# A gather kernel for a recommendation model: one field of five tiles fetched row by row from SyncE's queue, and layers and last steps in another order

## The reference

```python
sp_emb = emb_tables[fidx, sp_input]                      # 2048 x 26 x 32
lin_vals = lin_tables[fidx, sp_input, 0]
lin_output = ds_input @ lin_w.T + lin_b + jnp.sum(lin_vals, axis=1, keepdims=True)
s = jnp.sum(sp_emb, axis=1)
bi_pooled = 0.5 * (s * s - jnp.sum(sp_emb * sp_emb, axis=1))
x = jnp.concatenate([bi_pooled, ds_input], axis=1)       # 2048 x 45
h = jax.nn.relu(x @ w1.T + b1)                           # 256
h = jax.nn.relu(h @ w2.T + b2)                           # 128
out = jax.nn.sigmoid(h @ fw.T + fb + lin_output)
```

## Time and profile before

| | |
|---|---|
| median of 3 runs | 400.91 us (400.11 to 402.16) |
| the profiled execution, own time | 398.72 us |
| its span, first to last instruction | 396.9 us |
| mean granted TensorE clock | 0.993 |
| busy share: TensorE products, VectorE, GpSimd, ScalarE | 95%, 83%, 73%, 61% |
| gathers from GpSimd | 300, mean 956 ns |
| matching products | 1624 |

### The profile page before, as it was taken

One profiled execution on the slowest core, in us unless ns is written; L12 is line 12 of the kernel. 1 busy time (PEld: TensorE's weight loads), 2 busy tenths in 40 slices (PEclk: granted clock), 3 DMA queues, 4 the chain that ended last, 5 costly groups with the idle time before them and its releaser, 6 DMA issues.

```text
span 396.9 us, 5382 instructions
## 1 busy us (share of the span) xinstructions
PE 378.9 (95%) x1766; PEld 324.6 (82%) x1766; DVE 329.0 (83%) x336; ACT 240.3 (61%) x406; POOL 287.8 (73%) x310
## 2 busy tenths in 40 slices
PE   3999999999999999999999999999999988999884
PEld 2888888888888888888888888888888875767542
DVE  6799999979789796997979799697978995485952
ACT  5996865876376673875639756477665465322222
POOL 5777777777777777777777777777777777777740
PEclk9999999999999999999999999999999998999998
DMA  7733236332543327333273223633254222222210
GB/s 226 191 80 29 27 33 184 34 26 14 139 85 27 28 15 194 28 28 29 14 195 27 27 29 43 178 30 26 15 140 69 14 14 14 14 15 14 14 12 0
DMA packets 16900, 23.01 MB, mean 58 GB/s; under 512 B 6084, under 2 KB 15958, under 8 KB 15961
## 3 DMA queue, kind: packets, MB, share of 16 engines
q0 software_dynamic: 9600, 5.09, 22.9%
q1 hardware_dynamic: 7272, 17.58, 13.9%
HBM read 22.60 MB, written 0.04 MB: 57 GB/s over the span
## 4 chain that ended last, share of the span: by engine, by line
PE 92%; DVE 4%; ACT 2%; issue 1%; DMA 1%; ACTq 0%
PE cand L704 42%; PE cand L707 42%; PE bank_b L743 1%; PE bank_b L736 1%; PE bank_b L725 1%; PE bank_b L749 1%; PE bank_b L718 1%; PE bank_b L756 1%; DMA idx_raw<-sparse 1%; DVE sums L420 1%; PE cand L743 1%; PE cand L736 1%; ACT gates L562 1%; DVE last_picks L384 0%; DVE pick_sums L407 0%
## 5 line engine op out<-in xcount | busy, mean ns | idle before, releaser
L301 POOL DMA_INDIRECT rows<-table,row_idx x300 | 286.7, 956 | 94.1 <-issue 70.7
L704 PE MATMUL cand<-high,gates 128*128 128x462 f32 x812 | 308.3, 380 | 0.4 <-DVE gates L352 0.4
L707 PE MATMUL cand<-low,gates 128*128 128x462 f32 x812 | 304.2, 375 | 0.0
L704 PEld LDWEIGHTS cand<-high,gates 128*128 128x128 f32 x812 | 154.4, 190 | 23.2 <-issue 5.0
L707 PEld LDWEIGHTS cand<-low,gates 128*128 128x128 f32 x812 | 154.0, 190 | 20.4 <-issue 2.4
L384 DVE TENSOR_REDUCE picks<-masked 128x66 f32<-128x924 f32 x56 | 107.4, 1917 | 1.9
L378 DVE TENSOR_TENSOR masked<-cand,mask 128x924 f32<-128x924 f32 x57 | 63.7, 1118 | 42.3 <-PE cand L707 42.0
L562 ACT ACTIVATE gates<-distance,one 128x512 fp32r<-128x512 bf16 x116 | 76.9, 710 | 0.0
L554 ACT ACTIVATE distance<-codes,minus_key 128x512 bf16<-128x512 f16 x112 | 74.4, 712 | 0.0
L352 DVE TENSOR_SCALAR gates<-bank_a,key_of 128x512 fp32r<-128x512 f32 x87 | 59.9, 743 | 0.5 <-ACT bank_a L548 0.5
L529 ACT CAST high<-stage 128x462 fp32r<-128x462 f32 (+2 forms) x52 | 31.0, 596 | 33.4 <-DMA stage<-tabs 33.3
(11 more groups left out here) (91 smaller groups left out, 99.1 us busy)
## 6 DMA issues: line engine op xcount, KB each, us to landing
stage<-tabs SPq DMA_DIRECT2D x7, 1617.0 KB
rows<-table,row_idx POOLq DMA_INDIRECT x300, 3.2
codes<-codes_dram SPq DMA_DIRECT2D x28, 128.0 KB, 3.1
stage<-tabs SPq DMA_DIRECT2D x7, 231.0 KB, 4.2
idx_raw<-sparse SPq DMA_DIRECT2D x1, 208.0 KB, 2.5
w_sb<-w2t SPq DMA_DIRECT2D x1, 128.0 KB
xT<-dense_rows SPq DMA_DIRECT2D x1, 120.0 KB
w_sb<-w1x SPq DMA_DIRECT2D x1, 80.0 KB
```

The costliest lines, as they stand in the source:

```text
L301: pool.indirect_dma_start(out=rows[t % RING][:, g * W:(g + 1) * W], out_offset=None, in_=table[:, :], in_offset=bass.IndirectOffsetOnAxis( ...
L704: first = nc.tensor.matmul(to, gate, high[f % 2][:, k, :], start=(k == 0), stop=False)
L707: last = nc.tensor.matmul(to, gate, low[f % 2][:, k, :], start=False, stop=(k == CHUNKS - 1))
```

## The change

One field of tiles 3, 6, 8, 11 and 13 (the last one, field 25) is no longer gathered from GpSimd, so 295 gathers are left (`PF` counts them for each tile). SyncE fetches it instead, one sample's row at a time: 128 direct DMAs of 33 floats for a tile, with the row's number read into a register. They stand in pieces of 26 behind the loads of codes of jobs 5 to 28, and two more pieces behind the last load: 25 pieces, 640 DMAs. VectorE works out the row numbers in three small instructions at the start, from a sixth small input of 5 x 128 numbers. ScalarE and VectorE wait for a second semaphore at each tile. Apart from that, ScalarE's order in jobs 26 to 28 and the order of the last steps on ScalarE, VectorE and TensorE are other ones, and the last tile's rows are cut after 13 of 18 fields and no longer after 15. The rule that holds gathers back keeps its numbers.

```diff
+    BY_ROW = [3, 6, 8, 11, 13]
+    PF = [GF[t] - (t in BY_ROW) for t in range(TILES)]
+    ROWS_AT = [5, 11, 16, 21, 26]
+    TURN_ROWS = 26
...
-    SPLIT = GF[LAST] - 3
+    SPLIT = GF[LAST] - 5
...
+            sp.dma_start(one_raw[:, :], singles).then_inc(one_in, 16)
             sp.wait_ge(codes_out, 16)
...
+            def load_rows(n, p0):
+                t = BY_ROW[n]
+                if p0 == 0:
+                    sp.wait_ge(one_step, 3)
+                    if t >= RING:
+                        sp.wait_ge(reduced, 2 * (t - RING + 1))
+                p1 = min(p0 + TURN_ROWS, P)
+                _, at = nc.values_load_multi_w_load_instructions(
+                    one_idx[n:n + 1, p0:p1], engines=[mybir.EngineType.SP], min_val=0, max_val=F * CATS - 1,
+                    skip_runtime_bounds_check_because="one_idx is clamped")
+                for p in range(p0, p1):
+                    sp.dma_start(rows[t % RING][p:p + 1, PF[t] * W:GF[t] * W], table[bass.DynSlice(at[p - p0], 1), :]
+                                 ).then_inc(one_by_one[t % RING], 16)
+            turns = {ROWS_AT[n] + p0 // TURN_ROWS: (n, p0) for n in range(len(BY_ROW)) for p0 in range(0, P, TURN_ROWS)}
...
                     load_codes(j)
+                    if j in turns:
+                        load_rows(*turns[j])
+            for j in range(NJ, max(turns) + 1):
+                load_rows(*turns[j])
...
-                for g in range(GF[t]):
-                    n = sum(GF[:t]) + g
+                for g in range(PF[t]):
+                    n = sum(PF[:t]) + g
...
+            dve.wait_ge(one_in, 16)
+            nc.vector.tensor_scalar(one_wrap[:, :], one_raw[:, :], 0, CATS, ALU.is_lt, ALU.mult).then_inc(one_step, 1)
...
                     dve.wait_ge(gathered[t % RING], gathered_until(t))
+                    dve.wait_ge(one_by_one[t % RING], rows_until(t))
...
                 act.wait_ge(gathered[t % RING], gathered_until(t))
+                act.wait_ge(one_by_one[t % RING], rows_until(t))
```

More of the change, by code:

```diff
@@ L5, with build_deep_fm @@
 from contextlib import ExitStack
-def build_deep_fm(nc, dense_rows, sparse, cols, table, tabs, w1x, w2t, b2c, fwc, wlx, out):
+def build_deep_fm(nc, dense_rows, sparse, cols, singles, table, tabs, w1x, w2t, b2c, fwc, wlx, out):
     fp32 = mybir.dt.float32
@@ L84, in build_deep_fm, with rows_until @@
     LAST = TILES - 1
-    SPLIT = GF[LAST] - 3
+    SPLIT = GF[LAST] - 5
     def gathered_until(t):
-        return 16 * sum(GF[u] for u in range(t % RING, t + 1, RING))
+        return 16 * sum(PF[u] for u in range(t % RING, t + 1, RING))
+    def rows_until(t):
+        return 16 * P * sum(u in BY_ROW for u in range(t % RING, t + 1, RING))
     def codes_until(j):
@@ L104, in build_deep_fm @@
     LET = [0] + list(itertools.accumulate(19 if j in HIDDEN else 12 for j in range(NJ) for _ in range(TB * len(HALVES))))
-    assert 10 * AHEAD + LET[-1] > 10 * sum(GF)
+    assert 10 * AHEAD + LET[-1] > 10 * sum(PF)
     def begun_until(n):
@@ L137, in build_deep_fm @@
         col_code = sb("col_code", [R, P], fp16)
+        one_raw = sb("one_raw", [len(BY_ROW), P], i32)
+        one_wrap = sb("one_wrap", [len(BY_ROW), P], i32)
+        one_idx = sb("one_idx", [len(BY_ROW), P], i32)
         codes = [sb(f"codes{k}", [P, N], fp16) for k in range(3)]
@@ L220, in build_deep_fm @@
         gathered_end = sem("gathered_end")
+        one_in = sem("one_in")
+        one_step = sem("one_step")
+        one_by_one = [sem(f"one_by_one{k}") for k in range(RING)]
         squared = sem("squared")
@@ L479, in _ @@
             make_mask(0, 1)
+            dve.wait_ge(one_in, 16)
+            nc.vector.tensor_scalar(one_wrap[:, :], one_raw[:, :], 0, CATS, ALU.is_lt, ALU.mult).then_inc(one_step, 1)
+            dve.wait_ge(one_step, 1)
+            nc.vector.scalar_tensor_tensor(one_wrap[:, :], one_raw[:, :], CATS - 1, one_wrap[:, :], ALU.min,
+                                           ALU.add).then_inc(one_step, 1)
+            dve.wait_ge(one_step, 2)
+            nc.vector.tensor_scalar(one_idx[:, :], one_wrap[:, :], 0, (F - 1) * CATS, ALU.max,
+                                    ALU.add).then_inc(one_step, 1)
             for j in range(NJ - 1):
@@ L513, in _ @@
             pick_last(2)
+            dve.wait_ge(gathered[LAST % RING], gathered_until(LAST) - 16 * (GF[LAST] - SPLIT))
+            sum_rows(LAST, LAST, 0, SPLIT)
             pick_last(3)
@@ L517, in _ @@
             relu1(BLOCKS - 1, 1)
-            dve.wait_ge(gathered[LAST % RING], gathered_until(LAST) - 16 * (GF[LAST] - SPLIT))
-            sum_rows(LAST, LAST, 0, SPLIT)
             dve.wait_ge(gathered_end, 16 * (GF[LAST] - SPLIT))
@@ L642, in _ @@
                     high_chunk(*CHUNK_AT[j, 0])
+                if j in HIDDEN:
+                    relu1(HIDDEN[j], 0)
                 if j - 1 in SUMMED_OF:
                     square_picks(SUMMED_OF.index(j - 1))
-                if j + 2 < NJ:
+                if j in HIDDEN:
+                    relu1(HIDDEN[j], 1)
+                elif j + 2 < NJ:
                     make_gates(j + 2, FIRST_ACT, ACT_GATES)
-                if j in HIDDEN:
-                    relu1(HIDDEN[j], 0)
                 if j in CASTS:
@@ L656, in _ @@
                     high_piece(f, PIECE[g], PIECE[g + 1])
-                if j in HIDDEN:
-                    relu1(HIDDEN[j], 1)
                 if (j, 1) in CHUNK_AT:
@@ L663, in _ @@
                 if j in HIDDEN:
+                    if j + 2 < NJ:
+                        make_gates(j + 2, FIRST_ACT, ACT_GATES)
                     relu2(HIDDEN[j])
@@ L668, in _ @@
             relu1(BLOCKS - 2, 0)
-            square_last(0, 2)
             relu1(BLOCKS - 2, 1)
             square_tile(LAST - 1)
+            square_last(0, 2)
             relu2(BLOCKS - 2)
             square_last(2, 3)
+            act.wait_ge(gathered[LAST % RING], gathered_until(LAST) - 16 * (GF[LAST] - SPLIT))
+            square_rows(LAST, LAST, 0, SPLIT)
             sigmoid(BLOCKS - 2)
@@ L677, in _ @@
             relu1(BLOCKS - 1, 0)
[L678 to L681, removed]
             act.wait_ge(gathered_end, 16 * (GF[LAST] - SPLIT))
             square_rows(LAST, LAST + 1, SPLIT, GF[LAST])
+            relu2(BLOCKS - 1)
             square_sums(BLOCKS)
+            sigmoid(BLOCKS - 1)
             relu1(BLOCKS, 0)
@@ L715, in turn, with turn_picks @@
             def turn(m, t, parts):
+                turn_picks(m, t)
+                return turn_rows(m, t, parts, parts[-1])
+            def turn_picks(m, t):
                 c = slice(t % TB * P, (t % TB + 1) * P)
@@ L722, in turn, with turn_rows @@
                     nc.tensor.matmul(TOTAL[m][0:V, c], last_picks[:, i, :], ident[:, :], start=False, stop=False)
+            def turn_rows(m, t, parts, end_of):
+                c = slice(t % TB * P, (t % TB + 1) * P)
                 for at in parts:
@@ L725, in turn @@
                     last = nc.tensor.matmul(TOTAL[m][0:V, c], sums[:, at, :], ident[:, :], start=False,
-                                            stop=(at == parts[-1]))
+                                            stop=(at == end_of))
                 return last
@@ L806, in _ @@
             linear(3)
-            layer2(3)
-            layer3(3)
             pe.wait_ge(y_made, BLOCKS - 1)
             pe.wait_ge(picked, PAIRS + 1)
-            turn(4, LAST, [LAST, LAST + 1]).then_inc(folded, 1)
+            turn_picks(4, LAST)
+            turn_rows(4, LAST, [LAST], LAST + 1)
+            layer2(3)
+            turn_rows(4, LAST, [LAST + 1], LAST + 1).then_inc(folded, 1)
+            layer3(3)
             layer1(4, 0)
@@ L846 @@
         "cols": np.ascontiguousarray(sp[:, :M].T).reshape(M * (B // P), P),
+        "singles": np.ascontiguousarray(sp[:, F - 1].reshape(B // P, P)[[3, 6, 8, 11, 13]]),
         "table": both.reshape(F * C, E + 1),
```

## The result

| | before | the change |
|---|---|---|
| median of 6 runs | 400.83 us | 450.75 us |
| ratio, 95% interval | | 1.124 (1.121 to 1.127) |
| profiled execution, own time; span | 398.72; 396.9 us | 450.94; 448.8 us |
| first fold of block 0 to the last `sigmoid` | 75.8 us | 70.2 us |

The account below looks back on a forecast made before the run. It took TensorE, 95% busy, as the bound, with GpSimd's gathers a second chain as long. Terms of -4.9, -1.5 and -2.2 us made -8.6 us, from 400.91 to 392.3 us, range 389.5 to 404.

Parts of the forecast that it names:

- Terms 1 and 2: Jobs 26 and 28: `relu1` ahead of gates and of the squares of `last_picks` shortens TensorE's waits; -4.9 and -1.5 us.
- the end of the products: Job 28 on TensorE: the last matching product ends at 373.3 us instead of 379.7.
- Term 3: Gathers and last steps at the kernel's end: five gathers less and the new order save 2.2 us.
- The price on SyncE: SyncE's list: 26 rows at 0.37 us plus a 1.0 us load make a 10.6 us piece, which fits, costing nothing.
- rival A: SyncE becomes the bound and tables come late; the gain is eaten at 12.0 us a piece; slower, chance 0.21.
- its formula: Table lateness from field 3 to field 7 for pieces of T us: 17 T - 187; beyond 9 us TensorE pays.
- That small transfers cost nothing: 640 one-row DMAs beside GpSimd's gathers: transfers overlap, so they were costed at nothing.
- the limit for late tables: Tables for ScalarE: up to 9 us late is made up by idle time on ScalarE and VectorE, costing nothing.
- the point where SyncE stops fitting: SyncE's list of four jobs against 47.13 us between table loads: stops fitting at a piece of 11.3 us.

Follow-up runs that it names:

- fixed rows: The change with 640 one-row fetches of constant row numbers, no register loads or address steps (field 25's look-up left out): 390.00 us against 400.69 before.
- ScalarE's order alone: The kernel before with only ScalarE's order in jobs 26 to 28 changed, last steps as before, 300 gathers: 394.64 us against 400.58.
- layers and last steps: The kernel before with the change's whole order of layers and last steps, last tile cut after 13 fields, no row fetches: 398.82 us against 400.69.
- even pieces: The change with pieces of 28, 28, 24, 24 and 24 rows, so register loads begin at multiples of 16 bytes: 420.88 us, ratio 1.050 to before.
- the kernel with three tiles: The change with only tiles 3, 6 and 12 by row, in pieces of 24 or 20 rows, 297 gathers: 396.24 us against 400.69 before.
- the kernel with four tiles: The change with tiles 5, 8, 11 and 14 by row from job 10 on, pieces of 24 or 20, 296 gathers: 393.28 us against 400.58 before.

## Why the prediction was wrong

**Terms 1 and 2 and the end of the products** were right where the tables are in time. With fixed rows the folds of blocks 0 and 2 stand 38.2 us apart (318.79 to 356.95; 43.0 before), and the products end at 373.0, forecast 373.3. The last `sigmoid` came 9.3 us earlier than before, forecast 8.6. ScalarE's order alone brought 5.9 us.

**Term 3** came out in the rows of the kernel with fixed rows, where the last gather starts at 375.2; no run had 295 gathers with the old last steps, so what the new ones are worth there is not shown. What I had not seen is that it is a loss without them: from 394.6 (layers alone) to 398.8 us (layers and last steps) with 300 gathers. I wrote that less than term 3 would remain if only the products ended earlier; it was less than nothing for the new order of the last steps, some 2.7 us of it by the clock level.

**The price on SyncE is the step that failed**, by two terms of its sum. I took a row at 0.37 us: 0.228 and 0.04 came as taken, but the address step was 0.14 us in place of 0.10, for there are two instructions, the second of which I had not counted. That is 1.0 us a piece. And I took the load of registers at 1.0 us: it was 1.6 to 2.0 us where it starts at a multiple of 16 bytes and 5.5 where not, 3.3 in the mean, 2.3 us a piece more. The rest of the difference are rows at up to 0.43 us. The upper bound of 3.2 us for this load was wrong too, as 5.5 lies far above it. The bounds of a whole piece (7 and 24 us) held; the value between them, 10.6, was 14.3. The mechanism stood in rival A with its place (the tables), the point at which it decides (12.0 us a piece) and a chance of 0.21. With 14.3 its formula gives 56 us of lateness at field 7 and some 439 us; 66 us and 450.75 were measured. With the even pieces' 12.6 us it gives 27 us and 410.5 us; 37 us and 420.88 were measured. So it has the slope right (29 us for 1.7 us a piece, 29.9 measured) and is 10 us too low in both. Of the 10 us of lateness that it lacks in the change, 5 were there at field 3 already, as field 2's table was 11.3 us late and the formula begins with one wait at field 3; 3.1 more are a second wait, which it does not have, of the piece of tile 11 for VectorE to sum tile 7 (until 255.7). That the rows alone would have turned the sign is not shown: at 0.41 us with a load of 1.0 they make a piece of 11.7 us, below the formula's 12.0, but the formula is too low where it can be checked.

**That small transfers cost nothing** was right (fixed rows, 0.974), and so was the limit for late tables in its order of size: 8.4 us late cost 3.3 us, so that 9 us for nothing was too generous. In the change itself this limit decided little, since the tables were 11 to 66 us late.

The rule of the Trainium skill that I weighed ("DMA: Bandwidth & Descriptors", section "Why a DMA increments its semaphore by 16 and not by 1", 512 sequencer cycles for a DMA instruction on generations before the newest; with the 1.2 GHz of "Advanced Engine Details and Errata", "Clock Domains", an estimate of 0.43 us) reached the right sign for a reason that the trace does not bear out: the issue took 0.228 us. The Trainium skill's page "DMA: Bandwidth & Descriptors", section "Latency and other measured facts", gives about 600 ns as the floor of a tensor load. This case agrees that it is a floor: 1.38 us were the least for 20 registers, in the kernel with three tiles. I had left it out of the sum, where 0.6 in place of 1.0 would have made the piece shorter still.

The chance was the weaker choice. My value for a piece lay 0.7 us below the point where SyncE stops fitting and 1.4 below the one that decides the sign, and two of its three unknown terms were hardly bounded at all (0 to 0.3 us for the address step, 0.04 to 3.2 us for the load). That is nearer to an even chance than to 0.21.

## What to carry to other kernels

When work moves to an engine that "only issues DMAs", write that engine's list as a budget per period and count every instruction of it, register loads and address arithmetic too; one that fills 94% of the period on guessed prices, as here (44.2 of 47.13 us), can as well be the bottleneck. Measure the load of registers before its price goes into a sum, and let it start at multiples of 16 bytes. And an order of last steps is worth what the arrival times make it: the one that belongs to the 390.0 us with 295 gathers lost 4 us with 300, so such moves are to be tried apart.

## What the runs showed of the hardware

- A load of registers from SBUF on SyncE took 1.39 us for 20, 1.61 for 24 and 1.84 for 28, some 0.056 us a register. For 26 that began at a multiple of 16 bytes it took 2.0 us, 0.3 above that line, and for 26 that began 8 bytes past a multiple 5.48 us. Why 26 lies above the line was not tried.
- A one-row DMA whose address is in a register took 0.228 us to issue, as the plain one of line 273 did; with its two address instructions it was 0.41 us from start to start. With a constant address the issue was 0.252 us (median, 0.223 to 0.599) and 0.30 to 0.32 from start to start.
- 640 one-row transfers beside 295 gathers disturbed neither much: a gather took 955 ns and landed after 3.2 us, as before (956 ns, 3.2), and the first cast of a table started 7.4 to 9.7 us after its issue (before: 7.2 to 9.2).
- Near the end `layer2(3)` took 2.76 us, the lower clock level, in the kernel with four tiles, where TensorE had idled for 2.2 us before the products of `layer1(3)`, and 1.46 us with fixed rows, where it had idled for 2.3. Which of the two comes was not settled.
